# Attention and low-rank FFN block on one core: tile 4's softmax weights transposed by VectorE through DRAM, tile 5's transposes behind tile 7's scores

## What is computed

```python
h = layernorm(x) * (1 + ca) + sa
q = (h @ wq).reshape(B, T, 32, 128)      # k and v: 8 heads of 128
q, k = rope(q), rope(k)
scores = einsum('bhtd,bhsd->bhts', q, k) / sqrt(128)
att = softmax(where(tril, scores, -inf))
out = einsum('bhts,bhsd->bhtd', att, v)
x = x + ga * (out.reshape(B, T, 4096) @ wo)
h = layernorm(x) * (1 + cb) + sb
y = h @ W.T + b + lora(h)                # rank 8, 16, 32 or 64, chosen per token
x = x + gb * y
```

## Time and profile before

| | us |
|---|---|
| median of 3 runs (1050.92 to 1054.93) | 1053.05 |
| the profiled execution | 1053.54 |
| its span in the trace | 1051.8 |
| busy in the span: PE, DVE, ACT, POOL | 1029.1, 777.3, 633.8, 527.5 |

### The profile page before, as it was taken

How to read it: one execution, slowest core, us unless ns; L and a number is a source line. 1 busy time by engine, 2 the same in 40 slices (tenths; PEclk the granted TensorE clock), 3 DMA queues, 4 the chain that set the end, 5 groups by cost and what they waited for, 6 DMA issues and landing times.

```text
span 1051.8 us, 16408 instructions
## 1 busy us (share of the span) xinstructions
PE 1029.1 (98%) x5330; PEld 852.7 (81%) x5330; DVE 777.3 (74%) x1862; ACT 633.8 (60%) x1322; POOL 527.5 (50%) x505
## 2 busy tenths in 40 slices
PE   6999999999999999999999999999999999999998
PEld 3678888888888888888888888888888888888776
DVE  5778875788668875688758876688758875788566
ACT  5567763587447764478447764487546764478433
POOL 4536562466336663366425653365535653465233
PEclk9999999999999999999999999999999999999999
DMA  8363323223402323122302233133312233023001
GB/s 304 88 222 97 106 60 81 65 77 91 110 1 72 115 76 80 59 83 91 98 14 71 91 101 80 37 94 92 82 38 71 81 99 92 23 94 86 1 22 60
DMA packets 98284, 86.90 MB, mean 83 GB/s; under 512 B 39380, under 2 KB 84052, under 8 KB 98072
## 3 DMA queue, kind: packets, MB, share of 16 engines
q1 hardware_dynamic: 97384, 85.75, 27.6%
q10 hardware_dynamic: 816, 0.10, 0.1%
HBM read 59.23 MB, written 26.61 MB: 82 GB/s over the span
## 4 chain that ended last, share of the span: by engine, by line
PE 67%; DVE 10%; ACT 8%; issue 7%; POOL 6%; DMA 1%; SPq 0%; POOLq 0%; DVEq 0%; ACTq 0%
PE accumulators L722 17%; PE accumulators L707 15%; PE scores L632 11%; PE accumulators L684 11%; PE transposed L645 6%; ACT p_large L949 3%; POOL p_small L1668 3%; DVE pb_lo L1284 2%; PE scores L912 2%; POOL p_large L1668 2%; DVE p_small L1268 2%; ACT qr L984 2%; PE accumulators L745 1%; POOL qc L1685 1%; ACT pb_hi L958 1%
## 5 line engine op out<-in xcount | busy, mean ns | idle before, releaser
L1668 POOL TENSOR_SCALAR p_large<-p_large,rowinv 128x640 f32<-128x640 f32 (+3 forms) x128 | 127.4, 995 | 184.7 <-DVE rowinv L1273 184.7
L1677 POOL TENSOR_TENSOR qr<-qr,trig 128x512 f32<-128x512 f32 x80 | 111.8, 1397 | 197.0 <-ACT qr L984 197.0
L958 ACT ACTIVATE pb_hi<-transposed 128x512 fp32r<-128x512 f32 (+3 forms) x256 | 117.6, 498 | 134.8 <-PE transposed L645 134.4
L949 ACT ACTIVATE p_large<-p_large,negmax 128x640 f32<-128x640 f32 (+3 forms) x128 | 126.5, 988 | 85.3 <-DVE negmax L1268 83.2
L1284 DVE TENSOR_TENSOR pb_lo<-transposed,pb_hi 128x512 fp32r<-128x512 f32 (+3 forms) x256 | 140.0, 568 | 48.3 <-ACT pb_hi L958 47.5
L1668 POOL TENSOR_SCALAR p_small<-p_small,rowinv 128x128 f32<-128x128 f32 (+3 forms) x128 | 96.5, 770 | 80.7 <-DVE rowinv L1273 80.7
L1268 DVE CUSTOM_DVE_ANT_0 p_large<-scores,mask 128x640 f32<-128x640 f32 (+3 forms) x128 | 128.8, 1015 | 10.7 <-PE scores L632 5.8
L632 PE MATMUL scores<-k_hi,q_hi 128*128 128x512 f32 (+2 forms) x352 | 135.3, 384 | 0.0
L632 PE MATMUL scores<-k_hi,q_lo 128*128 128x512 f32 (+2 forms) x352 | 122.8, 349 | 0.0
L632 PE MATMUL scores<-k_lo,q_hi 128*128 128x512 f32 (+2 forms) x352 | 122.1, 347 | 0.0
L645 PE MATMUL transposed<-ident,p_large 128*128 128x128 f32 x832 | 113.4, 274 | 5.5 <-POOL p_large L1668 4.7
(11 more groups left out here) (193 smaller groups left out, 2257.4 us busy)
## 6 DMA issues: line engine op xcount, KB each, us to landing
p_rows<-turned SPq DMA_DIRECT2D x31, 640.0 KB, 3.1
pa_lo<-p_rows SPq DMA_DIRECT2D x124, 160.0 KB, 3.1
stage<-in_L_attn_wq_dram SPq DMA_DIRECT2D x32, 256.0 KB, 2.8
stage<-in_L_attn_wo_dram SPq DMA_DIRECT2D x32, 256.0 KB, 3.0
v_rows<-vt SPq DMA_DIRECT2D x32, 128.0 KB, 2.7
v_lo<-v_rows SPq DMA_DIRECT2D x32, 128.0 KB, 3.1
y<-in_L_wmod_dram SPq DMA_DIRECT2D x4, 512.0 KB, 6.6
stage<-in_L_attn_wk_dram SPq DMA_DIRECT2D x8, 256.0 KB, 2.7
```

Of the source, the lines that this page charges most:

```text
L949: nc.scalar.activation(row(i), row(i), ACT.Exp, bias=negmax[:, i:i + 1], scale=-1.0, accum_out=rowsum[:, i:i + 1]).then_inc(s_exp, 1)
L958: nc.scalar.activation(pt_of(i, part, True), src, ACT.Copy).then_inc(t_hi, 1)
L1668: nc.gpsimd.tensor_scalar(row(i), row(i), rowinv[:, i:i + 1], 1.0, ALU.mult, ALU.mult).then_inc(s_norm, 1)
L1677: nc.gpsimd.tensor_tensor(qr[:, s, :], qr[:, s, :], trig[:, 1, half * HALF:(half + 1) * HALF], ALU.mult).then_inc(r_sin, 1)
```

## The change

Three things, of which the first is the largest.

1. **Tile 4 leaves TensorE's transposes in 31 of the 32 heads** (all but the last). VectorE turns its 128 x 640 row in one instruction (`turn_four`), into `turned` for the first head and into `vt` for all others. The SP queue stores it to `four_rows` and reads it back in four pieces into `pb_lo`, right after the same head's `turn_columns`. In the next head's `front`, ScalarE copies it to `pb_hi` (`four_hi`) ahead of tile 7's copies, and VectorE subtracts (`four_lo`). The pb buffers become `[128, 4, 28, 32]`, so that the matmul, ACT and DVE address them in runs of 32 elements. Tile 6's mask now waits for `turn_four`, and `transposes(h, 5)` stands behind `scores(h, 7)`.
2. **Places within the heads**: in the last head of a group, tile 4's mask goes ahead of two of the block transposes, and a second swap of halves goes ahead of `early_hi` on ScalarE; in head 0 the second half of k is rounded before tile 3's exponential; in head 2 `split_hi(("wo", 2))` goes ahead of `early_hi`.
3. **The tail**: the transposed FFN weight `("W", 2)` comes before `weighted(3, 0)`, `("W", 3)` before scores 7; the masks, exponentials and splits are reordered to match; `low_rank` stacks the two halves of its left operand on 128 rows and makes two products in place of three (ScalarE writes a second copy of `fb_hi` once).

```diff
 class Numbers: (back)
-        self.banks(h, 4, g)
         self.step("s", (h, 6), g)
...
-        pb_hi, pb_lo = sb("pb_hi", [P, 26, P], F32R), sb("pb_lo", [P, 26, P], F32R)
+        pb_hi, pb_lo = sb("pb_hi", [P, 4, 28, 32], F32R), sb("pb_lo", [P, 4, 28, 32], F32R)
...
+            def turn_four(n):                       # SP queue
+                sp.wait_ge(p_turned, turn_count(n, 4))
+                if n:
+                    sp.wait_ge(four_in, 64 * n)
+                sp.dma_start(four_rows, four_turned(n)).then_inc(four_out, 16)
+                sp.wait_ge(four_out, 16 * (n + 1))
+                if n:
+                    sp.wait_ge(a_full, N.of[("a", ("pvb", (n - 1) % R), (n - 1) // R)])
+                src = four_rows.rearrange("(a c) (b m) -> b c a m", a=4, b=4)
+                for b in range(4):
+                    dst = f32(four_blocks(pb_lo)[32 * b:32 * b + 32]).rearrange("p a l r -> p a (l r)")
+                    sp.dma_start(dst, src[b]).then_inc(four_in, 16)
...
                 turn_columns(R * g + 1)
+                turn_four(R * g + 1)
                 load(("wo", 1), at)
...
 TensorE, back(h):
                 fill(h, 4, at)
-                transposes(h, 4, at)
                 scores(h, 6, at)
+                scores(h, 7, at)
                 transposes(h, 5, at)
-                scores(h, 7, at)
                 fill(h, 5, at)
...
 low_rank:
-                for n, (a, b) in enumerate(((tm_hi(s), fb_hi), (tm_hi(s), fb_lo), (tm_lo(s), fb_hi))):
-                    mm = nc.tensor.matmul(S[:, s, :], a, b, start=False, stop=(n == 2))
-                mm.then_inc(f_full, 1)
+                nc.tensor.matmul(S[:, s, :], tm_hi(s), fb_lo, start=False, stop=False)
+                nc.tensor.matmul(S[:, s, :], tm_stack(s), fb_twice, start=False, stop=True).then_inc(f_full, 1)
...
 ScalarE, front(h):
                     output_hi(hb, 0, at, ahead)
+                    four_hi(hb, at, ahead)
                 fill(h, 1, at)
...
+            def four_hi(h, at, ahead):
+                n = head_number(h, at, ahead)
+                act.wait_ge(four_in, 64 * (n + 1))
+                nc.scalar.activation(four_blocks(pb_hi), f32(four_blocks(pb_lo)), ACT.Copy).then_inc(four_hi_done, 1)
...
 VectorE, front(h) and back(h):
                 masked(h, 1, at)
+                    four_lo(hb, at, ahead)
                     output_lo(hb, 0, at, ahead)
...
-                transposed_lo(h, 4, at)
+                turn_four(h, at)
                 masked(h, 6, at)
...
+            def turn_four(h, at):
+                n = head_number(h, at)
+                need(dve, s_norm, N.value("s", (h, 4), at))
+                if n:
+                    dve.wait_ge(v_out, 64 * (at.g + 1))
+                    dve.wait_ge(four_out, 16 * n)
+                else:
+                    dve.wait_ge(rows_out, 16)
+                nc.vector.transpose(four_turned(n).rearrange("p (b l r) -> p l b r", b=4, r=32),
+                                    row(4).rearrange("p (j b c) -> p j b c", b=4, c=32)).then_inc(p_turned, 1)
+
+            def four_lo(h, at, ahead):
+                dve.wait_ge(four_hi_done, head_number(h, at, ahead) + 1)
+                nc.vector.tensor_tensor(four_blocks(pb_lo), f32(four_blocks(pb_lo)), f32(four_blocks(pb_hi)),
+                                        ALU.subtract).then_inc(four_lo_done, 1)
```

More of the change, by code:

```diff
@@ L353, in adaln_block @@
         pa_hi_done, pa_lo_done = sem("pa_hi_done"), sem("pa_lo_done")
+        four_out, four_in, four_hi_done, four_lo_done = (sem(n) for n in ("four_out", "four_in", "four_hi_done", "four_lo_done"))
         a_full, a_hi, a_swapped, a_taken = sem("a_full"), sem("a_hi"), sem("a_swapped"), sem("a_taken")
@@ L676, in weighted @@
                              (t_lo, second, hi_lo, range(4, 8))]
+                    n = head_number(h, at, ahead) + 1
+                    if n <= LAST:
+                        pe.wait_ge(four_hi_done, n)
                 single = 4 * half + 3
@@ L679, in weighted @@
                     pe.wait_ge(done, count)
+                    if half and done is t_lo and count == first and n <= LAST:
+                        pe.wait_ge(four_lo_done, n)
                     for v, hi in products:
@@ L1050, in back @@
                 exp(h, 5, at)
-                if at.first and not h:
-                    fill(h, 4, at)
-                    transposed_hi(h, 4, at)
-                else:
-                    transposed_hi(h, 4, at)
-                    fill(h, 4, at)
+                fill(h, 4, at)
                 if h == 0:
@@ L1081, in back @@
                 exp(h, 7, at)
+                if last:
+                    fill(h, 5, at, slice(1, 2))
                 if h in (0, 3):
@@ L1085, in back @@
                     transposed_hi(h, 6, at)
-                fill(h, 5, at, slice(1 if last else 0, None))
+                fill(h, 5, at, slice(2 if last else 0, None))
                 if last:
```

79 lines of the change are left out of this document (50 added, 29 removed).

## The result

| | before | after |
|---|---|---|
| median, us (4 runs each, side by side) | 1052.01 | 1038.80 (1037.79 to 1041.42) |
| ratio, 95% interval | | 0.9875 [0.9857, 0.9893] |
| the profiled execution, its span | 1053.54, 1051.8 | 1037.79, 1035.3 |
| busy: PE, DVE, ACT, POOL | 1029.1, 777.3, 633.8, 527.5 | 1013.5, 799.4, 628.3, 533.8 |

The change gains 13.2 us by the medians and 15.8 us between the two profiled executions, where 27.2 had been forecast. The direction is right, the size is half. 1038.8 us lies inside the stated range (1015 to 1045) but outside the forecast's own case (1021 to 1031); it lies in that of rival 1 (1034 to 1047), which had been given 0.20.

A forecast was written before the change was run, and what follows sets the result against it. The prediction took TensorE, busy 1029.1 of 1051.8 us, as the bound. Transposes 16.7, waits 6.5 and tail 4 made 27.2 us less, so 1026 us, with a range of 1015 to 1045.

The forecast's parts named there:

- the forecast's own case: Whole kernel: 1026 us expected, the case spanning 1021 to 1031 us, given a chance of 0.48.
- rival 1: Short heads 1 and 2 become bound by VectorE and ScalarE, only long heads gain: 1041 us (1034 to 1047), chance 0.20.
- The transposes, 16.7 us: Tile 4's transposes leaving TensorE save 0.54 us a head in 31 heads, 16.7 us.
- Runs of 32 in pb, "nothing": Products from pb in runs of 32 elements cost nothing, at most 5.6 us over 32 heads.
- The waits, 0.9 us a group: TensorE's waits in a group of four heads shrink by net 0.9 us, 6.5 us in 7.5 groups; bounds 0 and 13.
- new: `weighted`, front of head 3: In the front of head 3 TensorE newly waits about 0.7 us for ScalarE's copy of tile 7.
- each is costed by what is queued behind it: Replacement work on other engines: VectorE gets 0.66 us more a head and still fits a short head by 1.4 us.
- The DMAs, nothing: Tile 4's store and four reads a head, 20 MB more, cost nothing; 1.3 us to spare in head 1.
- The tail, 4 us: After the heads: shorter wait before `project_out(0)`, half of 0.9 us clock loss back, fewer `low_rank` products; 4 us, between 1 and 6.
- `low_rank`'s 1.8 us: In the tail, one product of 0.23 us fewer in each of 8 tiles saves 1.8 us on TensorE's path.
- the subtraction that gets in GpSimd's way: `four_lo` slows GpSimd's rotation sum in the fronts of heads 2 and 3, costing 6.5 us: 1033 us, chance 0.10.
- rival 3: Tile 4's reads come back late in the fronts of heads 2 and 3, TensorE stands: slower, 1067 us, chance 0.06.

The follow-up runs named there:

- the landing buffer: The change with tile 4's reads landing in their own tile, from which the copy and subtraction write pb in its old contiguous layout: 1036.76 us, 0.9837 of before.
- the tail alone: The kernel before with only the change's tail (W 2 earlier, W 3 ahead of mask 7, `low_rank` in two products): 1050.67 us, 0.9981 of before.
- the loads behind the store: As the weights behind the turns, with the loads waiting for that low half moved from ahead of pa's store to behind it: 1037.99 us, 0.9864 of before.
- the weights behind the turns: The change with VectorE's low half of the next wq moved behind the turns and mask 4 in heads 1 and 2: 1081.9 us, 1.0288 of before.

## Why the prediction was half right

**The transposes, 16.7 us: right.** In head 0, where nothing is waited for, the route takes 43.01 to 42.57 us, and with the landing buffer, so without the price of the layout, to 42.47: 0.54 us, the price in the forecast's sum.

**Runs of 32 in pb, "nothing": wrong.** It is the step that read a row of the last keys for all of them. 0.13 us a head is 4.2 us of TensorE, inside the upper bound of 5.6, and 1.6 to 2.0 us of the kernel's time.

Mask 6 does stand right behind scores 6: in the head 1 above it starts 1.59 us after them (1.45 forecast).

```profile
321.80 1.09 DVE L1309 CUSTOM_DVE_ANT_0 p_large<-scores,mask 128x896 f32<-128x896 f32 x1 [0.55 <-PE scores L662]
```

**The waits, 0.9 us a group: wrong by half.** 4 x 0.54 for the transposes and 4 x 0.13 for the layout leave 2.02 - 2.16 + 0.52 = 0.4 us a group for the waits, 3 us in all for 6.5. Term by term, each read as in the prediction from the distance between starts (means of the five groups, us a group):

| | forecast | measured |
|---|---|---|
| gone: tile 6 in head 1 | 0.34 | 0.11 |
| gone: tile 4 in head 2 | 0 | 0.22 |
| gone: tile 4 in head 3 | 0.55 | 0.61 |
| gone: v in head 3 | 0.42 | 0.41 |
| gone: tile 7 in front of head 3 | 0.30 | 0.07 |
| new: `weighted`, front of head 3 | -0.70 | -0.52 |
| new: `weighted`, front of head 2 | 0 | -0.28 |
| new: pa at the end of head 2 | 0 | -0.31 |

The first two lines are a matter of the group that was read: the third has its wait in head 1 (0.44 us), the others 0.16 us there and 0.22 or more ahead of tile 4's transposes in head 2. Tile 7's wait in front of head 3, forecast at 0.1, stayed at 0.33 us. What failed above all is the step "each is costed by what is queued behind it": it asked whether VectorE has room for `four_lo` in a short head, and it has; it did not follow what stands behind it. Tile 7's copies and low halves do, behind the new copy and `four_lo`: the new wait was named for the front of head 3 and not for that of head 2. And the turns of tiles 0 to 3 do, the start of a roundtrip of some 8 us on which ScalarE, and TensorE behind it, wait in head 2. The earlier trace rows had the warning: 2.9 us of waiting for that DMA before the change already. It is rival 1 in one head of four, by a mechanism that the rival didn't name; head 1 kept its gain, head 3 gained 1.0 us, and that the time lies near rival 1's 1041 us is luck.

**The DMAs, nothing: right for tile 4**, whose copy waits for no DMA and whose transfers left out bring nothing. The second group's 2.2 us belong to pa's roundtrip, and late reads of it came in single groups of most runs, without tile 4's transfers too.

**The tail, 4 us: 2.0 (1.2 to 2.9).** The wait went from 2.06 to 0.85 us as forecast. The clock gave back more than half of 0.9: the loss was 1.6 us over all twelve products, of which I had counted the first four, and all of it came back (4.45 to 2.85 us, at a granted clock of 1.00). But `low_rank`'s 1.8 us turned into waits for VectorE in the last three tiles, and the change itself has another wait in the front of the last head, so that from its start to the end of the span there are 98.6 us before, 95.9 with the tail alone and 96.7 in the change.

The 16.5 us between the two profiled spans lie here: 1.1 us ahead of the first head, 2.2 in the first group, nothing in the second, 10.1 in the next five, 1.2 in heads 0 to 2 of the last and 1.9 from the last head on. The first of these is no gain of the change's: in the runs built on the change that point lies anywhere from 39.5 to 41.3 us. By terms, 16.7 - 4.2 + 3 + 1.9 for the tail - 2.2 for the second group + 1.1 for the start make 16.3. Of the rivals, the subtraction that gets in GpSimd's way is there, GpSimd's sum took 1.80 us beside `four_lo` in heads 2, but ScalarE's copy of its result there came without idle time: no run here charges it with anything, and none left it out by itself. Tile 4 is not late, so rival 3 falls.

## What to carry to other kernels

Cost a new instruction by what stands behind it in its queue, and above all by the first thing there that starts a long chain such as a DMA roundtrip, not by whether its engine has room. Where two chains end at nearly the same time, as pa's copy and GpSimd's sum do here, shortening one returns next to nothing. And when an instruction moves, look at what else waits for it, the DMA queue's loads included. Where an engine waits in some heads and not in others, a saving counts in full only in the others: a price of 0.13 us a head came to half of it or less at the end. Price an access pattern from the row with the same shape, since the pattern that is free for short products need not be free for long ones.

## What the runs showed of the hardware

- Four fp32r products of 128x512 took 0.91 us from start to start with a contiguous moving row and 0.94 to 0.95 us where it comes in runs of 32 elements (128 bytes), with little difference between steps of 128 and of 896 bytes.
- A 128x4 operation of VectorE between SBUF tiles took 1.25 us in place of 0.23 where GpSimd's 128x512 addition had begun just before, and both ended together; in these rows of the tail of the change GpSimd's starts at 1011.49 and ends at 1012.77:

```profile
1011.49 1.28 POOL L1856 TENSOR_TENSOR y<-y,qc 128x512 f32<-128x512 f32 x1
1011.54 1.25 DVE L1684 TENSOR_SCALAR gs<-gs 128x4 f32<-128x4 f32 x1
```

  The Trainium skill, page "SBUF — State Buffer", section "Who interferes with whom", says that where VectorE, in a mode with two ports that `tensor_scalar` can enter, and GpSimd contend, the one that issues first holds the shared ports for its whole instruction and the other waits. The trace agrees as to who waits and how long; that this operation ran in that mode no run here shows. The operation was held until GpSimd's ended, and the run that moved the addition took 0.5 us off the mean of this operation.
- Pa's store and four reads, up to the copy that waits for them, took from 7.7 to 8.4 us in head 2 of seven groups of the change and 9.4 in one, and once (the loads behind the store) the copy started 5.2 us after the last read's issue, where it is 2.9 to 3.7 us in those seven groups. A wait that rests on a roundtrip has to be read over several groups.
- Behind a wait of TensorE of 2.8 us (the weights behind the turns) the granted clock was 0.50 over the next 3.2 us, and behind one of 2.06 us (the tail before) 0.62 over 4.45 us; behind the waits of 0.85 us it was 1.00.
